# Attention on a Trainium2: masks multiplied on GpSimd, other products paced by the exponential of the step ahead, one Q half kept back

## The chip, the cores and the metric

One Trainium2 chip, eight cores, one program on all of them. Core number 4b+c works on batch b and on every fourth token from token c on, 1024 query tokens in all. The cores exchange nothing. The time is that of the slowest core, in microseconds (us) of the device.

## The reference, cut to what matters

```python
q = jnp.einsum('bse,hed->bhsd', x, Wq) + bq[None, :, None, :]      # 16 heads of 128
kg = jnp.einsum('bse,ged->bgsd', x, Wk) + bk[None, :, None, :]     # 4 groups
vg = jnp.einsum('bse,ged->bgsd', x, Wv) + bv[None, :, None, :]
k, v = jnp.repeat(kg, 4, axis=1), jnp.repeat(vg, 4, axis=1)
scores = jnp.einsum('bhqd,bhkd->bhqk', q, k) * (1.0 / np.sqrt(d))
scores = jnp.where(causal[None, None, :, :], -jnp.inf, scores)
attn = jax.nn.softmax(scores, axis=-1)
out = jnp.einsum('bhqk,bhkd->bhqd', attn, v)
# x = layernorm(x + out), with x of shape (2, 4096, 2048)
# x = fwht(x * SU_ug) / 64; silu(x @ W_gate.T * ..) * (x @ W_up.T * ..)
# x = fwht(x * SU_dp) / 64; x @ W_down.T * ..; layernorm(x + that)
```

## The kernel before, in words

Five stages follow each other on each core. K and V of the whole batch are projected first (until about 250 us), then comes attention (about 255 to 667 us), then the up and gate products with the second transform, then the down product with the last norm.

**Attention** runs in 384 steps. A head has two halves of 512 queries (`hf` 0 and 1). Half 0 has 8 steps, half 1 has 16; a step P takes 256 keys. The order of the halves is head after head, with (14, 0), (15, 0), (14, 1), (15, 1) at the end (`halves`, line 397). In the last 8 steps of each half the causal edge passes through the tile: step r of them (r = 0 to 7) works on the last 512-64r queries only. Step i of the program issues, in this order on TensorE:

- S(i): two score products of up to 512 columns (`emit_S`, line 418), into one of two pairs of PSUM banks. S(i) waits for the exponential of step i-2. ScalarE then takes the exponential of both (line 437), 1024 columns in a full step.
- O(i-3): the products of the probabilities with V (`emit_O`, line 454), up to eight of 129 columns; the last column sums the row. `LO` = 3 is the lag.
- "other products" (`run_items`, line 604), as many as a budget allows. Each step adds a quota to the budget, each product takes 1.0 off it.

After TensorE's part of a step comes, on the program's list, `out_bank` (line 472) where a pair of query tiles is finished (r = 3 and r = 7): VectorE's reciprocal, two multiply-adds, for r = 7 a cast, and two statistics. Then `emit_mask(i)` (line 441): 64 columns of each score tile are multiplied by the mask on VectorE (line 451), and for odd r GpSimd zeroes 64 more (line 449). O(i) waits for these.

**The other products** come from two queues. The plain one holds the projections of the Q halves still to come, 16 products of 512 columns each (`q_item`); Q of head h may start at the first step of head h-2. The `fast` one holds for each finished half a transpose (T: four products of 128 columns, `tr_mm`) and at least three steps after it the first transform (F: one product, `f1_mm`). These items use PSUM banks 6 and 7 in turn, so the first product of an item waits until VectorE has emptied the bank of the item before the last (`free[bk]`; line 371 for Q, 518 for T, 528 for F). Each engine works its list in order. Once the first halves of all heads are done, the statistics of the norm (`norm_A`) and 16 pairs of products with the stage matrix (`st1_mm`, emptied by line 585) join the queue. GpSimd's list also holds the loads of the weights of Q (line 359) and of up and gate (`ug_load`, line 633), which wait for TensorE to let go of the place. The first load of up and gate is issued when Q of (15, 1) is done.

## Time and profile before

| | us |
|---|---|
| median of 3 runs (2090.55 to 2092.16) | 2091.55 |
| the profiled execution | 2087.97 |
| its span, slowest core | 2086.9 |
| the eight cores' spans | 2077.2 to 2086.9 |
| TensorE busy in the span | 2021.6 (97%) |
| ScalarE, VectorE, GpSimd busy | 488.4, 566.4, 149.2 |

The profile is of one execution; TensorE is busy nearly always, and the chain of work that ended last runs 88% over it. Busy time of TensorE is partly modelled: products overlap, so a run of products is best read by its start and the start of what comes next. A wait is put down to the engine whose signal came last.

### The profile page before, as it was taken

To read this page: it belongs to the slowest core of one execution; us is meant where nothing else is said; L and a number is where in the kernel's file an instruction comes from. 1 tells how busy PE (TensorE), PEld (TensorE's weight loads), DVE (VectorE), ACT (ScalarE), POOL (GpSimd) and SP (SyncE) were. 2 spreads that over 40 slices of the span, in tenths; PEclk is the share of its full clock that TensorE was granted. 3 is DMA by queue.
4 is the path that set the end of the run, shared out by engine and by line. 5 is a ranking of instruction groups with operands and counts; after the bars stand their busy time and mean duration, and the time that the engine had idled before them with its cause. 6 is when DMAs were issued, how large, how long until landed. Compare 5 with 4: busy or idle time off the path is not lost.

```text
span 2086.9 us, 30398 instructions; the slowest of 8 cores (2077.2 to 2086.9 us)
## 1 busy us (share of the span) xinstructions
PE 2021.6 (97%) x11760; PEld 1043.6 (50%) x11760; DVE 566.4 (27%) x1334; ACT 488.4 (23%) x639; POOL 149.2 (7%) x364
## 2 busy tenths in 40 slices
PE   5999999999998999999999999999998999999997
PEld 2444466666665444444444444444444754444456
DVE  0111144445556412212212212122122530303033
ACT  0110088777785101001001001001002410000002
POOL 3000000000000000000000000000000000000001
PEclk9999999999999999999999999999999999999999
DMA  9885133333325355455455455455453743747359
GB/s 153 140 129 94 30 62 77 72 72 73 81 55 92 61 97 98 84 97 97 84 98 96 84 98 96 84 98 94 85 98 79 127 105 70 159 81 156 73 126 311
DMA packets 92812, 207.00 MB, mean 99 GB/s; under 512 B 11776, under 2 KB 51712, under 8 KB 87680
## 3 DMA queue, kind: packets, MB, share of 16 engines
q0 software_dynamic: 34816, 141.74, 39.3%
q1 hardware_dynamic: 57856, 63.32, 10.8%
q8 instruction: 97, 1.59, 0.3%
q14 instruction: 43, 0.35, 0.1%
HBM read 294.31 MB, written 24.12 MB: 153 GB/s over the span
## 4 chain that ended last, share of the span: by engine, by line
PE 88%; DMA 5%; DVE 2%; ACT 2%; issue 1%; POOL 1%; DVEq 0%; SPq 0%; ACTq 0%; POOLq 0%
PE PS L181 88%; DMA AR<-xkv 2%; ACT AR L437 2%; DMA AR<-scr_h 1%; DMA scr_h<-wmt 1%; POOL AR L219 1%; DMA AR<-WdownP 1%; DMA out<-AR 0%; DVE AR L484 0%; DVE AR L451 0%; DMA AR<-AR 0%; DVE AR L371 0%; DVE stat L882 0%; DVE stat L495 0%; DVE AR L528 0%
## 5 line engine op out<-in xcount | busy, mean ns | idle before, releaser
L181 PE MATMUL PS<-AR 128*128 128x512 bf16 (+4 forms) x11296 | 1979.0, 334 | 45.6 <-DMA AR<-WkT 21.0
L181 PEld LDWEIGHTS PS<-AR 128*128 128x128 bf16 x11296 | 1005.0, 98 | 994.5 <-issue 87.3
L437 ACT ACTIVATE AR<-PS,negc 128x1024 bf16<-128x1024 f32 (+7 forms) x384 | 322.8, 865 | 100.3 <-PE PS L181 91.1
L786 ACT ACTIVATE AR<-PS,sgate 128x512 bf16<-128x512 f32 x128 | 88.0, 687 | 825.5 <-PE PS L181 825.5
L790 DVE SCALAR_TENSOR_TENSOR AR<-PS,scombo,AR 128x512 bf16<-128x512 f32 x128 | 96.1, 751 | 445.4 <-ACT AR L786 445.4
L741 DVE CAST AR<-PS 128x512 bf16<-128x512 f32 x128 | 88.5, 692 | 276.0 <-PE PS L181 276.0
L635 POOL DMA_DIRECT2D AR<-WupT x64 | 33.8, 529 | 838.2 <-PE PS L181 838.2
L451 DVE TENSOR_TENSOR AR<-AR,maskb 128x128 bf16<-128x128 bf16 x256 | 52.3, 218 | 117.7 <-ACT AR L437 117.5
L891 DVE TENSOR_TENSOR a_b<-PS,AR 128x512 f32<-128x512 f32 (+1 forms) x16 | 9.7, 622 | 271.5 <-PE PS L181 267.8
L1000 ACT ACT_TABLE_LOAD x1 | 1.3, 1283 | 349.3 <-DVE mv L998 349.3
L276 DVE TENSOR_TENSOR AR<-PS,AR 128x512 bf16<-128x512 f32 x32 | 21.8, 690 | 221.0 <-PE PS L181 221.0
L271 ACT ACTIVATE AR<-PS,bkc 128x512 bf16<-128x512 f32 x32 | 21.7, 687 | 164.2 <-PE PS L181 164.2
L181 PE MATMUL PS<-AR,st 128*128 128x512 bf16 x160 | 53.7, 387 | 2.3 <-DVE AR L585 2.3
L845 DVE CAST AR<-PS 128x512 bf16<-128x512 f32 x64 | 44.1, 690 | 35.5 <-PE PS L181 35.5
L848 ACT CAST AR<-PS 128x512 bf16<-128x512 f32 x64 | 37.4, 586 | 52.8 <-PE PS L181 52.8
L181 PE MATMUL PS<-AR,h 128*128 128x512 bf16 x128 | 48.8, 381 | 0.0
L755 POOL DMA_DIRECT2D AR<-WdownP x32 | 16.9, 532 | 435.9 <-PE PS L181 398.5
L484 DVE SCALAR_TENSOR_TENSOR AR<-PS,rcp,AR 128x128 f32<-128x128 f32 x128 | 39.1, 346 | 8.5 <-DVE rcp L477 3.6
L449 POOL MEMSET AR<- 128x128 bf16 x128 | 25.2, 210 | 214.5 <-PE PS L181 214.4
L371 DVE TENSOR_SCALAR AR<-PS,bqc 128x512 bf16<-128x512 f32 x32 | 24.0, 749 | 43.1 <-PE PS L181 43.1
L636 POOL DMA_DIRECT2D AR<-WgateT x64 | 34.2, 534 | 3.1 <-issue 2.9
L495 DVE BATCH_NORM_STATS2 stat<-AR 128x6 f32<-128x128 f32 x128 | 30.9, 283 | 3.7 <-DVE AR L484 0.5
(72 smaller groups left out, 319.0 us busy)
## 6 DMA issues: line engine op xcount, KB each, us to landing
AR<-WupT POOLq DMA_DIRECT2D x64, 512.0 KB, 6.8
AR<-WgateT POOLq DMA_DIRECT2D x64, 512.0 KB, 11.0
AR<-WdownP POOLq DMA_DIRECT2D x32, 1024.0 KB, 10.2
AR<-AR SPq DMA_DIRECT2D x256, 64.0 KB, 4.9
AR<-xkv POOLq DMA_DIRECT2D x6, 2048.0 KB, 22.1
AR<-WqT POOLq DMA_DIRECT2D x16, 512.0 KB, 6.6
AR<-xtok SPq DMA_DIRECT2D x16, 512.0 KB, 4.3
scr_h<-AR SPq DMA_DIRECT2D x32, 256.0 KB, 2.3
```

Of the source, the lines that this page charges most:

```text
L181: return pe.matmul(o, lhsT, rhs, start=start, stop=stop, skip_group_check=True)
L437: et = p.inc(ac.activation(ebuf[:, :, cs:], sps[:, :, cs:], AF.Exp, bias=negc[:, 0:1], scale=INV_SQRT_D), "ac")
L451: e_tok[i][1] = p.inc(dv.tensor_tensor(ebuf[:, :, cs:cs + 64], ebuf[:, :, cs:cs + 64], mask2, ALU.mult), "dv")
L484: h1t = p.inc(dv.scalar_tensor_tensor(sl, ops[:, a, 0:D], rcp[:, 2 * ob + a: 2 * ob + a + 1], sl, ALU.mult, ALU.add), "dv")
L495: h1_half[n] = p.inc(dv.bn_stats(stat[:, o_:o_ + 6], x_[:, q * 128:(q + 1) * 128]), "dv")
L635: p.inc(gp.dma_start(wup[c % 3], WupT[c][:, :]), f"ug{c % 3}", 16)
L636: ug_tok[c] = p.inc(gp.dma_start(wgt[c % 3], WgateT[c][:, :]), f"ug{c % 3}", 16)
L741: free[bk] = t_ = p.inc(dv.tensor_copy(b1[s_], bank(bk)), "dv")
L786: at = p.inc(ac.activation(gsl[k], bank(2 + k), AF.Silu, bias=0.0, scale=sgate[:, c:c + 1]), "ac")
L790: t_ = p.inc(dv.scalar_tensor_tensor(av[k], bank(k), scombo[:, c:c + 1], gsl[k], ALU.mult, ALU.mult), "dv")
L845: acc_free[bk] = p.inc(dv.tensor_copy(bts(hf, j), bank(bk)), "dv")
L848: acc_free[bk] = p.inc(ac.copy(bts(hf, j), bank(bk)), "ac")
```

## The change

Three things are changed, all in attention. The mask product moves from VectorE's list to GpSimd's, behind the zeroing where there is one; O(i) then waits for one GpSimd signal. The quota is no longer a number between 1.15 and 1.70 but comes from `pace(i)`: an estimate of the exponential of step i-1, times `PACE` = 1.11, less an estimate of the step's own products, in units of one 512-column product; the last step of a half now runs its items at once too, where before it only saved its quota. And Q of (15, 1) may no longer start with head 13 but only with the half (14, 1).

```diff
-        LO = 3
+        LO, PACE = 3, 1.11
...
+                assert q_tok[h][hf]
                 p.w(pe, q_tok[h][hf])
...
-            e_tok[i] = [et, et, None]
+            e_tok[i] = [et, et]
...
             if r % 2:
                 p.w(gp, kv_done, o_tok[i - 6] if i >= 6 else None)
-                e_tok[i][2] = p.inc(gp.memset(ebuf[:, :, cs - 64:cs], 0.0), "pl")
-            p.w(dv, e_tok[i][0])
-            e_tok[i][1] = p.inc(dv.tensor_tensor(
-                ebuf[:, :, cs:cs + 64], ebuf[:, :, cs:cs + 64], mask2, ALU.mult), "dv")
+                p.inc(gp.memset(ebuf[:, :, cs - 64:cs], 0.0), "pl")
+            p.w(gp, e_tok[i][0], cw)
+            e_tok[i][1] = p.inc(gp.tensor_tensor(
+                ebuf[:, :, cs:cs + 64], ebuf[:, :, cs:cs + 64], mask2, ALU.mult), "pl")
...
+        def pace(i):
+            def cols(k):
+                return HT - steps[k][5] if 0 <= k < NS else 0
+            def tiles(k):
+                return 4 - max(steps[k][4], 0) // 2 if 0 <= k < NS else 0
+            if i >= NS:
+                return 0.0
+            exps = PACE * (0.26 + 0.83e-3 * 2 * cols(i - 1))
+            own = 2 * cols(i) * 0.42e-3 + 2 * tiles(i - LO) * 0.057
+            return max(0.0, (exps - own) / 0.2155)
...
-                q_item(h, hf, first_step[(max(h - 2, 0), 0)])
+                q_item(h, hf, first_step[(14, 1) if (h, hf) == (15, 1) else (max(h - 2, 0), 0)])
...
-            quota = 1.15 + 0.55 * (512 - steps[i][5]) / 512 if i < NS else 0.0
-            if i >= LO and steps[i - LO][7]:
-                emit_O(i - LO)
-                state["budget"] += quota
-            elif i > LO and steps[i - LO][6]:
+            quota = pace(i)
+            if i >= LO and steps[i - LO][6]:
                 emit_O(i - LO, (0,))
                 run_items(i, quota)
                 emit_O(i - LO, (1,))
```

How this moves instructions, at three places. First TensorE at the start of head 7's first half; 448, 384 and 320 columns are S of its steps 1 to 3, 129 columns are O, 512 columns a Q product. Before:

```order
L181 MATMUL PS<-AR 128x448 x2
L181 MATMUL PS<-AR 128x129 x2
L181 MATMUL PS<-AR 128x512 x2
L181 MATMUL PS<-AR 128x384 x2
L181 MATMUL PS<-AR 128x129 x2
L181 MATMUL PS<-AR 128x320 x2
L181 MATMUL PS<-AR 128x129 x4
L181 MATMUL PS<-AR 128x512 x3
```

Now:

```order
L181 MATMUL PS<-AR 128x448 x2
L181 MATMUL PS<-AR 128x129 x2
L181 MATMUL PS<-AR 128x512 x3
L181 MATMUL PS<-AR 128x384 x2
L181 MATMUL PS<-AR 128x129 x2
L181 MATMUL PS<-AR 128x512 x4
L181 MATMUL PS<-AR 128x320 x2
L181 MATMUL PS<-AR 128x129 x4
L181 MATMUL PS<-AR 128x512
```

Between S of 384 and S of 320 columns stood no Q product, now there are four.

Second VectorE in the middle of head 5, where the item Q of (6, 0) ends and F and T of earlier halves follow; L477 to L495 (L478 to L496 in the new numbering) are `out_bank`. Before:

```order
L477 RECIPROCAL rcp<-PS 128x2
L484 SCALAR_TENSOR_TENSOR AR<-PS,rcp,AR 128x128 x2
L495 BN_STATS stat<-AR 128x6 x2
L451 TENSOR_TENSOR AR<-AR,maskb 128x2x64
L371 TENSOR_SCALAR AR<-PS,bqc 128x512
L451 TENSOR_TENSOR AR<-AR,maskb 128x2x64
L528 CAST AR<-PS 128x512
L518 CAST AR<-PS 128x512
```

Now:

```order
L371 TENSOR_SCALAR AR<-PS,bqc 128x512
L478 RECIPROCAL rcp<-PS 128x2
L485 SCALAR_TENSOR_TENSOR AR<-PS,rcp,AR 128x128 x2
L496 BN_STATS stat<-AR 128x6 x2
L529 CAST AR<-PS 128x512
L519 CAST AR<-PS 128x512
```

The masks are gone, the emptying of Q's bank stands ahead of the `out_bank` group, and that of F's bank still behind it.

Third TensorE in the half (15, 0), steps 1 to 6. Before:

```order
L181 MATMUL PS<-AR 128x448 x2
L181 MATMUL PS<-AR 128x129 x2
L181 MATMUL PS<-AR 128x512 x2
L181 MATMUL PS<-AR 128x384 x2
L181 MATMUL PS<-AR 128x129 x2
L181 MATMUL PS<-AR 128x320 x2
L181 MATMUL PS<-AR 128x129 x4
L181 MATMUL PS<-AR 128x512 x3
```

Now:

```order
L181 MATMUL PS<-AR 128x448 x2
L181 MATMUL PS<-AR 128x129 x2
L181 MATMUL PS<-ident,AR 128x128 x2
L181 MATMUL PS<-AR 128x384 x2
L181 MATMUL PS<-AR 128x129 x2
L181 MATMUL PS<-AR 128x320 x2
L181 MATMUL PS<-AR 128x129 x8
L181 MATMUL PS<-AR 128x256 x2
L181 MATMUL PS<-AR 128x129 x8
L181 MATMUL PS<-AR 128x512
L181 MATMUL PS<-AR 128x192 x2
```

The 512-column products of Q (15, 1) have left this half; they now stand in (14, 1).

## Rows read from the trace of the kernel before

**Rows 1.** Spans of the cores: span from first to last instruction, granted clock.
```profile
core 0: 2085.2 us, clock 0.994
core 7: 2086.9 us, clock 0.993
```

**Rows 2.** Core 7 by stretch: length, then busy time and count per engine, clock.
```profile
250.00:670.00 420.00, 398.38 (x3786) 262.16 (x3784) 210.75 (x732) 323.22 (x386) 35.61 (x148) 0.99 0.34 76
720.00:1300.00 580.00, 580.00 (x2689) 262.99 (x2688) 117.64 (x164) 55.67 (x81) 43.34 (x83) 1.00 0.51 94
```

**Rows 3.** What TensorE waited for, 255 to 671 us, core 7: us, times, longest.
```profile
PE PS L181 <- DVE AR L451: 8.9, 12, 2.1
PE PS L181 <- ACT AR L437: 7.1, 22, 1.4
PE PS L181 <- DVE AR L371: 2.0, 6, 0.5
PE PS L181 <- DVE AR L585: 1.8, 1, 1.8
```

**Rows 4.** Groups by shape in attention: busy us, mean ns of one, idle before.
```profile
L437 ACT ACTIVATE AR<-PS,negc 128x1024 bf16<-128x1024 f32 x160 | 174.5, 1113 | 59.0 <-PE PS L181 58.9
L437 ACT ACTIVATE AR<-PS,negc 128x128 bf16<-128x128 f32 x32 | 11.8, 367 | 8.4 <-PE PS L181 6.2
L181 PE MATMUL PS<-AR 128*128 128x512 bf16 x853 | 244.5, 381 | 5.3 <-DVE AR L451 3.1 <-ACT AR L437 1.4 <-DVE AR L528 0.2
L181 PE MATMUL PS<-AR 128*128 128x129 bf16 x2304 | 198.4, 220 | 4.3 <-DVE AR L451 3.7 <-DVE AR L484 0.3
L451 DVE TENSOR_TENSOR AR<-AR,maskb 128x128 bf16<-128x128 bf16 x256 | 52.3, 218 | 117.7 <-ACT AR L437 117.5
L449 POOL MEMSET AR<- 128x128 bf16 x128 | 25.2, 210 | 214.5 <-PE PS L181 214.4
L359 POOL DMA_DIRECT2D AR<-WqT x16 | 8.5, 531 | 226.9 <-PE PS L181 226.9
```

**Rows 5.** Timeline, head 7: start, us, engine, instruction, idle before and releaser.
```profile
438.22 5.18 PE L181 MATMUL PS<-AR 128*128 128x320 bf16 x56 [0.30 <-ACT AR L437]
...
442.35 0.75 DVE L371 TENSOR_SCALAR AR<-PS,bqc 128x512 bf16<-128x512 f32 x1 [0.33 <-PE PS L181]
...
444.95 0.68 DVE L528 CAST AR<-PS 128x512 bf16<-128x512 f32 x1
445.55 0.21 DVE L451 TENSOR_TENSOR AR<-AR,maskb 128x128 bf16<-128x128 bf16 x1
...
445.77 2.64 PE L181 MATMUL PS<-AR 128*128 128x512 bf16 x8 [2.14 <-DVE AR L451]
```

**Rows 6.** Timeline, head 5, in the middle between its halves.
```profile
391.09 0.17 DVE L477 RECIPROCAL rcp<-PS 128x2 f32<-128x2 f32 x1
...
392.14 0.49 DVE L495 BATCH_NORM_STATS2 stat<-AR 128x6 f32<-128x128 f32 x2
...
392.67 0.74 DVE L371 TENSOR_SCALAR AR<-PS,bqc 128x512 bf16<-128x512 f32 x1
...
393.56 0.33 PE L181 MATMUL PS<-ident,AR 128*128 128x128 bf16 x3 [0.99 <-DVE AR L451]
```

**Rows 7.** Timeline, head 6: a mask and the product that waits for it.
```profile
419.13 0.21 DVE L451 TENSOR_TENSOR AR<-AR,maskb 128x128 bf16<-128x128 bf16 x1
...
419.48 0.27 PE L181 MATMUL PS<-AR 128*128 128x129 bf16 x2 [0.76 <-DVE AR L451]
```

**Rows 8.** Timeline, half (14, 1) and the end of attention.
```profile
639.89 2.79 PE L181 MATMUL PS<-AR 128*128 128x448 bf16 x30 [1.38 <-ACT AR L437]
...
666.26 0.61 PE L181 MATMUL PS<-AR 128*128 128x129 bf16 x4 [1.76 <-DVE AR L451]
...
669.52 0.59 PE L181 MATMUL PS<-AR,st 128*128 128x512 bf16 x1 [1.79 <-DVE AR L585]
```

**Rows 9.** Core 7, 5 us of head 7, columns as in rows 2.
```profile
445.00:450.00 5.00, 4.22 (x18) 2.10 (x19) 2.09 (x7) 2.17 (x3) 0.00 (x0) 0.66 0.09 26
```

## The prediction

> **What bounds the kernel now.** I read the spans of the cores first, then busy time by stretch, then what TensorE waited for in attention, then the groups by shape, and last the timeline around the longest waits. Eight cores do equal work and differ by under 10 us; the slowest, core 7, has 2086.9, core 0 has 2085.2 [rows 1]. After attention TensorE is busy without a gap: 580.00 of 580 us, which also gives the pitch of a 512-column product, 580/2689 = 0.216 us [rows 2]. In attention it is busy for 398.4 of 420 us [rows 2]. The change adds and takes no product, so all it can win there is the 21.6 us of idle time, 1.0% of the span, and what the clock does. I price other products by their columns: O of 129 columns 0.054 us (the kernel's own figure is 0.057, which I use), S of 64 columns 0.027.
>
> The idle time has three parts. VectorE's masks are named for 8.9 us in 12 waits, ScalarE's exponentials for 7.1 in 22, the emptying of Q's bank for 2.0 in 6, and one wait of 1.8 stands at the end [rows 3]. ScalarE is busy for 323 of the 420 us [rows 2], so it is not the bound on average; a full exponential takes 1.11 us, the smallest 0.37 [rows 4], and a step of TensorE must hold that much work or TensorE waits two steps later.
>
> **Who is really waited for.** The name of the mask is wrong in more than half of the 8.9 us. In head 6 a mask ends at 419.13 + 0.21 = 419.34 and the O product starts at 419.48, 0.14 later [rows 7]: that is what a signal takes. In head 7 the mask ends at 445.76 and TensorE starts at 445.77, too soon for that signal; F's bank was emptied at 444.95 + 0.68 = 445.63, 0.14 before [rows 5]. The product that starts is the first of a Q item, and the bank it needs is F's. The same in head 5: L371 ends at 393.41, T starts at 393.56 [rows 6]. By shape, 3.7 of the 8.9 us stand before O products, which do wait for masks; 3.1 stand before 512-column products and the rest, 2.1, before transposes [rows 4], which wait for banks. So before: masks 3.7, banks 5.2 + 2.0 + 0.2 = 7.4, exponentials 7.1, the end 1.8.
>
> **Masks to GpSimd.** 256 products leave VectorE, 52.3 us of work [rows 4]; VectorE does not end the chain, so this counts only through who waited. No row shows a two-input product on GpSimd. Below, it costs no less than GpSimd's zeroing of the same 128 elements, 0.21; above, I bound it by twice GpSimd's longest instruction in the stretch, the issue of a weight load of 0.53, so 1.06 [rows 4]. I take 0.43, the zeroing plus VectorE's own product (0.21 + 0.22), since the op writes as the one and reads as the other. O(i) stands behind S(i+2), which itself waits for exponential i, and behind S(i+3); with the signals that leaves at least some 0.6 us after the exponential, so at 0.43 nobody waits. In the list the masks stand behind one weight load per head, whose wait for TensorE is over by then, and a load issues in 0.53 us; with a mask due each 0.4 to 1.1 us and three steps of lag this is hidden too. The waits before O go, 3.7 us, but for 0.4 at the very end, where mask and O follow the last exponential with nothing between: -3.3 us. At that end 1.76 is now shown because two masks stood behind `out_bank` [rows 8].
>
> The GPSIMD Engine Reference of the Trainium skill (Performance versus the Vector engine, elementwise) speaks against the move: about 2.6 cycles an element for two inputs against VectorE's one, roughly half VectorE's rate. By its figures I estimate 128 x 2.6 / 1.2 GHz = 0.28 us and some dispatch. By that rule too the product would be hidden and the sum would be the same; no row of before shows it.
>
> **Pacing.** In step 2 of a half nothing but S and one pair of O stood between two full exponentials: steps 1 and 2 of the first half held 0.92 + 0.44 us against exponentials of 1.11 and 1.0. Hence the wait of 0.30 before S of 320 columns in each first half [rows 5] and its like. Now three or four products stand there, 1.14 + 1.30 us in head 7. Of the 7.1 us I let go all but the first steps of attention (0.5) and the 1.38 of half (14, 1) [rows 8], which is halved because three queue items now reach it. It costs elsewhere: half (15, 0) loses its Q products. Its steps 1 to 7 hold 4.1 us of products against 5.5 of exponentials (seven of them, from 1.11 down to 0.47 in even steps of 0.107, [rows 4]), so 1.5 with the signals. Sum 0.5 + 0.7 + 1.5, rounded up to 3.0: -4.1 us.
>
> **The banks: what is late next.** Pacing also places T, F and Q anew, and here it loses. Take the middle of head 5, from the end X of the step that ends Q of (6, 0). Its bank is read 0.24 later (a product takes 0.38 [rows 4] against a pitch of 0.216, and a signal) and is free at 0.99. Then comes `out_bank`, which lasts from 391.09 to 392.63, 1.54 us [rows 6]: until 2.53. F's bank takes 0.68 [rows 5]: 3.21, and 0.14 for the signal: 3.35. TensorE reaches Q of (6, 1), which needs F's bank, after S and O and F (0.50), S and O (0.66), and S, O and T (0.77): 1.93. It waits 1.42 us. The same walk in the order of before puts T's wait at 0.92, and the trace has 0.99 [rows 6], so I trust it to 0.2 or so. For the other heads it gives: heads 1 and 2, where F, T and the next Q item now stand in one step, 1.0 each (before, F and Q were 2.2 us apart); head 3 1.2; head 4 1.4; head 6 1.0. Together 7.0. In heads 7 to 13 both Q's and F's bank are now emptied ahead of `out_bank`: T is 0.95 us behind a bank that takes 1.13, 0.18 each, 1.3 together, where before head 7 alone had 2.14 [rows 5]. The items in the second halves follow each other at 0.94 to 1.05 us against 1.05 to 1.13, 1.7 together. Sum 10.0 against 7.4: +2.6 us.
>
> **The end and the clock.** The 1.79 before the stage products is VectorE's emptying of banks behind `out_bank` [rows 8] and stays. On core 7 the granted clock was 0.66 in the five microseconds after the 2.14 wait [rows 9]: 3.4 us at 1.2 instead of 2.4 GHz, 1.7 us of work lost. My longest wait there is now 1.42, and after 1.38 and 0.99 before no such fall is in the stretch's rows, so I take it to be gone: -1.7 for core 7. Core 0, at 2085.2 without that loss, is then level with it.
>
> **Sum.** -3.3 - 4.1 + 2.6 - 1.7 = -6.5 us: span 2086.9 to 2080.4. The profiled execution took 2087.97, the median of the runs is 2091.55; I carry the difference over to the median: 2085.0.
>
> **Rivals.**
> 1. The banks get no worse. VectorE has 52 us less to do, and if `out_bank` starts or runs earlier than in my walk, or TensorE arrives later, the 7.0 us shrink towards 1. For it: the walk counts microseconds that hang on steps of 0.1; against: it met the 0.99. Gain 6.5 + 6 = 12.5: 2079.
> 2. Nothing is left of it: the waits in the middle of heads 1 to 6 reach 2 us each (a multiply-add that is late for its reciprocal), or the clock falls in them or in the thin half (15, 0), 1.7 us a time, twice. For it: 2.14 did bring a fall [rows 9]. +5.5: 2090.5.
> 3. GpSimd becomes the bound, and the kernel slower. Eight masks and four zeroings of 0.21 per half must fit in the eight steps' 6.6 us (1.11 times eight exponentials of 0.74 on average) and some 1.5 of lag. 8T + 0.84 = 8.1 at T = 0.91: below that price of a mask no throughput is lost, above it 8 us for each microsecond, in 32 halves. At the upper bound, 1.06, 1.2 us a half, 39 in all: 2124. Against it: 1.06 is five times either nearest row. If instead T lies between 0.6 and 0.9, single O products wait a tenth or two, and this joins rival 2.
> 4. The change does not pace as it says, because the items run out as before. The lists show otherwise in the first steps of the halves, so I give it nothing of its own.
>
> **How the numbers follow.** Forecast 0.50, with its own range 2081 to 2088.5; rival 1 0.20; rival 2 0.20; rival 3 0.06; 0.04 for slower by another way. What a measurement of this kernel can tell from no change is about 0.2%, 4.2 us, so faster is below 2087.4. Faster: 0.43 of the forecast's 0.50 and rival 1's 0.20, 0.63. Within: 0.07 and 0.17 of rival 2, 0.24. Slower: the remaining 0.13. The range 2077 to 2091.5 leaves out rival 3, the far end of rival 1 and part of rival 2.
>
> **What would show it.** In the waits of TensorE the mask's line should be nearly gone (under 1 us), ScalarE's line should be about 3 us with the longest pieces near 630 us in half (15, 0), and the emptying lines of Q's and F's banks should be named for some 10 us, with waits of 1.0 to 1.5 in the middle of heads 1 to 6 and under 0.3 in heads 7 to 13. GpSimd's product should have a mean of about 0.43. If that mean is over 0.9, or the waits of a head's middle are gone or at 2 us, the prediction is wrong at that step. Rows after attention should be as before, only earlier.

## The result, and the profile after

The changed kernel takes 2069.7 us, median of 4 runs (2068.67 to 2070.28), against 2091.53 (2090.55 to 2092.16): ratio 0.9899, 95% interval 0.9887 to 0.9911. It is 21.8 us faster. 6.5 were forecast, and 2069.7 lies below the range of 2077 to 2091.5. In some executions of either kernel the cores of one die run at a lower granted clock and take longer; they are left out of all times and stages here. The profiled execution took 2069.54; its cores have 2058.1 to 2068.5 us, and the slowest is now core 4, not 7.

Core 4 by stretch (columns as in rows 2):

```profile
250.00:670.00 420.00, 408.38 (x3834) 268.45 (x3833) 180.70 (x495) 326.95 (x390) 139.10 (x404) 0.99 0.32 77
720.00:1300.00 580.00, 580.00 (x2689) 262.91 (x2688) 117.11 (x163) 55.71 (x82) 43.32 (x82) 1.00 0.48 93
```

Against [rows 2] TensorE is busy for 10 us more of the 420, VectorE for 30 us less, GpSimd for 103 more. After attention nothing has changed. What TensorE still waited for between 250 and 675 us on core 4:

```profile
PE PS L181 <- DVE AR L529: 3.5, 7, 1.1
PE PS L181 <- DMA AR<-AR: 2.0, 1, 2.0
PE PS L181 <- DVE AR L586: 1.7, 1, 1.7
PE PS L181 <- ACT AR L438: 1.2, 3, 0.5
PE PS L181 <- DVE AR L371: 1.2, 3, 0.5
PE PS L181 <- DVE AR L485: 0.6, 2, 0.3
...
PE PS L181 <- POOL AR L452: 0.3, 1, 0.3
```

Against [rows 3]: masks 8.9 to 0.3, exponentials 7.1 to 1.2. The two groups on GpSimd, in attention:

```profile
L452 POOL TENSOR_TENSOR AR<-AR,maskb 128x128 bf16<-128x128 bf16 x256 | 110.7, 434 | 163.2 <-ACT AR L438 121.3 <-PE PS L181 38.3
L450 POOL MEMSET AR<- 128x128 bf16 x128 | 26.6, 208 | 0.0
```

434 ns is the price that the prediction took. The longer waits of TensorE, one by one (timeline, columns as in rows 5):

```profile
288.67 0.38 PE L181 MATMUL PS<-ident,AR 128*128 128x128 bf16 x4 [0.31 <-DVE AR L371]
289.30 2.00 PE L181 MATMUL PS<-AR 128*128 128x512 bf16 x10 [0.25 <-DVE AR L529]
...
363.39 0.81 PE L181 MATMUL PS<-AR 128*128 128x512 bf16 x3 [1.12 <-DVE AR L529]
...
604.20 0.60 PE L181 MATMUL PS<-AR 128*128 128x384 bf16 x4 [0.53 <-ACT AR L438]
605.10 1.11 PE L181 MATMUL PS<-AR 128*128 128x320 bf16 x8 [0.30 <-ACT AR L438]
...
629.97 0.38 PE L181 MATMUL PS<-AR,st 128*128 128x512 bf16 x1 [1.99 <-DMA AR<-AR]
...
651.64 0.58 PE L181 MATMUL PS<-AR,st 128*128 128x512 bf16 x1 [1.71 <-DVE AR L586]
```

The waits stand where they were forecast: before Q of the second half in the middle of a head (363.39, head 4), in the thin half (15, 0) (604.20, 605.10), and before the emptying at the end (651.64). One was not: the first stage product now comes so early that it waits 1.99 us for the DMA that scatters the F of the half before it.

**Measured by starts.** The shown waits of attention fell by some 9 us, which does not account for 21.8. So I took the *starts* of products instead of the idle time between records. A product of 512 columns starts 0.216 us after the one before [rows 2], but its record lasts 0.38 [rows 4], so a record ends about 0.165 after the engine could go on. The rows show each wait short by that much, and none below it. For each product of attention I took start less the start before less its columns' time (the gap before a product, mean of the six cores whose records are all there; us):

| | S, for the exponential | O | T, F, Q, for banks | end | sum | attention |
|---|---|---|---|---|---|---|
| before | 14.5 | 6.8 | 12.5 | 2.6 | 36.5 | 406.5 |
| changed | 4.7 | 2.5 | 10.1 | 5.0 | 22.2 | 391.3 |
| forecast, from the rows | 7.1 to 3.0 | 3.7 to 0.4 | 7.4 to 10.0 | 1.8 to 1.8 | | |

"End" stands for the products of the norm and the stage matrix; it includes waits behind the last O (1.9 us before), which the last column leaves out. The last column is the mean over the cores from the first product of attention to its last O. The stage ahead of it, from the first product of all, fell too: 248.7 to 243.2 us. So attention gave 15.2 us and the first stage 5.5, 20.7 together. The later stages agree to 0.6 each, and all that is left took 1.4 us longer: the mean span of the cores fell by 19.3 us between these two profiles, that of the slowest core by 18.4. The 21.8 is between medians; the profiled execution before, 2087.97, was 3.6 us below its median. The Perfetto Trace Analysis of the Trainium skill (Summary: the profiler window per engine type) says that TensorE's records end at an estimated end, and its opening note calls matmul busy time a bad metric since matmuls are pipelined. This trace agrees, with the 0.38 against 0.216.

### The profile page after: what moved, and what is told of

Same layout as the page of the kernel before. It is cut to its first block, busy times and chain, and to the rows that moved or that the text cites. A ratio compares the mean times of both kernels' runs of the same rounds, so it can differ in the third digit from the quotient of the medians.

```text
span 2068.5 us, 30358 instructions; the slowest of 8 cores (2058.1 to 2068.5 us)
## 1 busy us (share of the span) xinstructions
PE 2016.6 (97%) x11760; PEld 1043.9 (50%) x11760; DVE 527.7 (26%) x1078; ACT 489.7 (24%) x639; POOL 252.4 (12%) x620
## 4 chain that ended last, share of the span: by engine, by line
PE 91%; DMA 5%; DVE 2%; issue 1%; POOL 1%; ACT 0%; DVEq 0%; SPq 0%; ACTq 0%; POOLq 0%
PE PS L181 91%; DMA AR<-xkv 2%; DMA AR<-scr_h 1%; POOL AR L219 1%; DMA scr_h<-wmt 1%; DMA AR<-WdownP 1%; DMA out<-AR 0%; DMA AR<-AR 0%; DVE AR L529 0%; DVE stat L896 0%; DVE AR L371 0%; DVE AR L485 0%; ACT AR L438 0%; DVE a_b L914 0%; DVE wmt L914 0%
## 5 line engine op out<-in xcount | busy, mean ns | idle before, releaser
L452 POOL TENSOR_TENSOR AR<-AR,maskb 128x128 bf16<-128x128 bf16 x256 | 110.7, 434 | 163.2 <-ACT AR L438 121.3
L276 DVE TENSOR_TENSOR AR<-PS,AR 128x512 bf16<-128x512 f32 x32 | 21.8, 691 | 217.1 <-PE PS L181 217.1
L769 POOL DMA_DIRECT2D AR<-WdownP x32 | 16.9, 531 | 435.6 <-PE PS L181 435.6
L496 DVE BATCH_NORM_STATS2 stat<-AR 128x6 f32<-128x128 f32 x128 | 30.8, 282 | 3.3
L478 DVE RECIPROCAL rcp<-PS 128x2 f32<-128x2 f32 x64 | 10.7, 167 | 70.8 <-PE PS L181 70.8
```

The costliest lines, as they stand in the source:

```text
L452: e_tok[i][1] = p.inc(gp.tensor_tensor(ebuf[:, :, cs:cs + 64], ebuf[:, :, cs:cs + 64], mask2, ALU.mult), "pl")
L496: h1_half[n] = p.inc(dv.bn_stats(stat[:, o_:o_ + 6], x_[:, q * 128:(q + 1) * 128]), "dv")
```

## The experiments

All numbers of stages are means over the cores of one profile, by starts. "First" is the stage before attention; the last column counts instructions in TensorE's list, the program that the engine works through in order, waits included. "Late half" is Q of (15, 1) held back to (14, 1); "filler" is a small instruction that does nothing useful. Two profiles of the same kernel, before, differ by 0.7 us in the first stage and 0.4 in attention.

| kernel | first | attention | TensorE's list |
|---|---|---|---|
| before | 248.7 | 406.5 | 13246 |
| before, again | 249.4 | 406.9 | 13246 |
| masks on GpSimd alone | 245.0 | 403.1 | 13215 |
| pacing and late half alone | 249.7 | 405.0 | 13248 |
| changed, without the late half | 244.3 | 391.5 | 13213 |
| changed | 243.2 | 391.3 | 13210 |
| before, last mask on GpSimd | 250.3 | 406.7 | 13245 |
| before, zeroing three times | 250.2 | 406.4 | 13246 |
| changed, filler on VectorE | 245.0 | 392.9 | 13210 |
| the same, longer | 243.3 | 393.2 | 13210 |
| changed, 36 waits on TensorE | 249.4 | 391.6 | 13246 |
| before, wait for zeroing on VectorE | 243.7 | 406.8 | 13118 |
| changed, mask twice | 244.7 | 432.8 | 13210 |
| changed, mask in two halves | 242.6 | 392.1 | 13210 |
| filler that waits for the exponential | 244.8 | 396.1 | 13210 |
| the same, and O waits for it | 249.6 | 404.6 | 13376 |
| out_bank a step later | 243.8 | 389.3 | 13214 |
| and the last one behind the stage products | 243.4 | 388.9 | 13213 |
| two steps later, stage products later | 243.3 | 386.6 | 13213 |
| the same with PACE 1.25 | 244.2 | 396.3 | 13203 |

### The parts alone

The kernel before, unchanged, on the chip of the next three:

> The kernel before, unchanged, profiled once more. In the two profiles so far the first stage (first product to the start of attention, mean of the eight cores) took 248.7 us before and 243.2 us after, attention 406.5 and 391.3 us, though the change does not touch the first stage. If the 5.5 us of the first stage are chance, this profile has a first stage anywhere between 242 and 250 us, and attention again within 1 us of 406.5. If they belong to the kernel, the first stage is again 248 to 250 us.

2091.2 us, first stage 249.4: it belongs to the kernel and not to the execution.

```diff
 # before, masks alone
-            p.w(dv, e_tok[i][0])
-            e_tok[i][1] = p.inc(dv.tensor_tensor(
-                ebuf[:, :, cs:cs + 64], ebuf[:, :, cs:cs + 64], mask2, ALU.mult), "dv")
+            p.w(gp, e_tok[i][0], cw)
+            e_tok[i][1] = p.inc(gp.tensor_tensor(
+                ebuf[:, :, cs:cs + 64], ebuf[:, :, cs:cs + 64], mask2, ALU.mult), "pl")
```

> Only the mask products move to GpSimd; the quota and the start of Q (15, 1) are those of before. Theory 1 (pacing brings most): counted from start to start of the products, before has 36 us of waits in attention: 14.4 before score products, 6.5 before O, 12.5 at the banks of the other products, 2.6 at the end. The masks account for the 6.5 (down to 2.5) and for 1 to 2 of the banks: attention 400 to 402 us instead of 406.5, ratio 0.9975. Theory 2 (VectorE's relief brings most: with 52 us less in its list its banks come free early): attention 395 or less, ratio 0.994 or less.

Ratio 0.9948 (0.9935 to 0.9962). Attention fell by 3.4 us only.

```diff
 # before, with pace(i) and the late half of the change; the masks stay on VectorE
-            quota = 1.15 + 0.55 * (512 - steps[i][5]) / 512 if i < NS else 0.0
+            quota = pace(i)
```

> Only the pacing and the late Q (15, 1); the masks stay on VectorE. Theory 1: the waits before score products fall from 14.4 to about 5, those before O stay at 6 to 7, the banks stay near 12: attention 396 to 398 us, ratio 0.995. Theory 2: 403 or more, ratio 0.998 or more, since VectorE's list is as full as before.

Ratio 0.9989 (0.9980 to 0.9998). Attention fell by 1.5 us. The 403 or more of theory 2 was met here, but its 395 or less with the masks alone was not (403.1), and theory 1 missed both. So neither theory stands: neither half brings it. The longest listed waits of the two, core 4; masks alone, then pacing alone:

```profile
PE PS L181 <- ACT AR L437: 9.2, 29, 1.4
PE PS L181 <- DVE AR L371: 4.1, 10, 0.9
PE PS L181 <- DVE AR L528: 3.3, 4, 1.7
...
PE PS L181 <- POOL AR L451: 0.5, 1, 0.5
```

```profile
PE PS L181 <- DVE AR L452: 13.4, 21, 1.0
...
PE PS L181 <- ACT AR L438: 0.3, 1, 0.3
```

With the masks gone TensorE waits for the exponentials (by starts 16.9 us before S, 1.4 before O); with the pacing alone it waits for masks (2.3 before S, 22.3 before O). Each takes away the wait that would have hidden the other: 3.4 and 1.5 apart, 15.2 together. Some 18.5 of the 22.3 us stand before O of one step, r = 6: its mask is listed behind `out_bank` of r = 3, three steps earlier. How it stands in the second run (timeline, the middle of head 5, as [rows 6]):

```profile
389.56 0.37 ACT L438 ACTIVATE AR<-PS,negc 128x128 bf16<-128x128 f32 x1
...
390.19 0.16 DVE L478 RECIPROCAL rcp<-PS 128x2 f32<-128x2 f32 x1
...
391.23 0.49 DVE L496 BATCH_NORM_STATS2 stat<-AR 128x6 f32<-128x128 f32 x2
391.63 0.21 DVE L452 TENSOR_TENSOR AR<-AR,maskb 128x128 bf16<-128x128 bf16 x1
391.76 0.69 DVE L529 CAST AR<-PS 128x512 bf16<-128x512 f32 x1
391.99 0.27 PE L181 MATMUL PS<-AR 128*128 128x129 bf16 x2 [0.99 <-DVE AR L452]
```

The mask runs as soon as `out_bank` is through and ends at 391.84; O starts 0.15 later. It is the mask of r = 6; at 389.56 the exponential of r = 7 starts, so that of r = 6 was done, and the mask, 0.21 us of work, starts 2.07 us later than it could have, behind the emptying of Q's bank and `out_bank`.

```diff
 # changed, without the late half
-                q_item(h, hf, first_step[(14, 1) if (h, hf) == (15, 1) else (max(h - 2, 0), 0)])
+                q_item(h, hf, first_step[(max(h - 2, 0), 0)])
```

> The changed kernel, but Q of (15, 1) may start with head 13 as before. Theory 1: half (15, 0) has its Q products back and loses its waits before score products (1.5 to 2 us), half (14, 1) runs thin instead and gets a wait of 1.4 us or more there; the sum within 1 us of the changed kernel, 2069 to 2072 us. Rival: the late Q is what keeps TensorE's clock up at the end of (14, 1), where before a wait of 1.54 us stood; then this kernel is 2 to 4 us slower than the changed one.

2072.0 us, ratio 0.9913 (0.9887 to 0.9938), attention 391.5: the late half brings 0.2 us there, less than two profiles of one kernel differ by. The total is 2.3 us above the changed kernel's, as the rival has it, but 1.1 of them lie in the first stage, and the intervals of the two ratios overlap.

### What in the masks on VectorE cost it

```diff
 # changed; filler on VectorE at the mask's place (0.06 us each)
+            p.w(dv, rcp_free[0])
+            rcp_free[0] = p.inc(dv.memset(rcp[:, 0:2], 1.0), "dv")
             p.w(gp, e_tok[i][0], cw)
```

> The changed kernel, with one small memset of two columns on VectorE in the place where each of the 256 mask products stood; GpSimd keeps the masks. Theory A (the kind on GpSimd) and theory B1 (the length of GpSimd's list): the first stage stays at 243 to 245. Theory B2 (the shorter list of VectorE decides): 248 to 250. In attention it measures what it costs to keep VectorE's list at its old length with only some 0.06 us of work an instruction: if what the change won came from the exponentials that VectorE no longer has to wait for in its list (a mask cannot be taken before its exponential), the filler, which waits for no exponential, costs at most 2 us of the 15.3: attention 391 to 394.

2074.0 us, ratio 0.9912 (0.9891 to 0.9934); attention +1.6, within the 391 to 394 expected.

```diff
 # the filler waits for the exponential, as the mask did
-            p.w(dv, rcp_free[0])
+            p.w(dv, e_tok[i][0], rcp_free[0])
```

> The changed kernel, masks on GpSimd, with a small memset (0.06 us) on VectorE in the place of each mask, which now waits for the exponential of its step as the mask did; nothing waits for the memset. The same memset without that wait left attention at 392.9 us. Masks on VectorE with the new pacing took 405.0. Theory H (VectorE standing before an exponential holds up the emptying of banks and out_bank behind it, and that was half of what the masks cost): attention 396 to 400, with the waits for Q's, T's and F's banks grown from 10 us to 14 or more. Theory M (it was the mask that was late, behind out_bank in VectorE's list, with TensorE's O waiting for it): attention 392 to 394, banks within 1 us. First stage 243 to 245 by both, as TensorE's list keeps 13210 instructions.

Ratio 0.9930 (0.9901 to 0.9959); attention 396.1, +3.2 more. The time is that of theory H, its place is not: the waits for Q's, T's and F's banks rose by 0.7 us only, those before O by 3.3. They stand before the first O of a half (by starts 1.6 us in the run before this one, 4.7 now), which waits until `out_bank` has read the O bank of an earlier half: VectorE, standing before an exponential, holds up `out_bank`. That is the mechanism of theory H, at another bank.

```diff
 # and O waits for the filler
+            e_tok[i].append(rcp_free[0])
```

> As the last one, and O of the step waits for VectorE's memset as it waited for the mask there; GpSimd still does the masks, so VectorE has 0.06 us an item in place of 0.22. Theory M: TensorE's O waits for VectorE's list again, attention 402 to 405, with 18 to 22 us before O products; what the move to GpSimd won is then that the signal for O no longer stands behind out_bank, and not VectorE's 52 us of work. Theory W (it was the work of 0.22 us each): attention 393 to 396. TensorE's list is 13376 instructions long by these waits, so by the finding of the earlier runs the first stage should be 248 to 251.

Ratio 0.9992 (0.9980 to 1.0004): the whole gain is gone though GpSimd does every mask. Attention 404.6, 21.3 us before O, 16.7 of them at r = 6; theory M holds. Core 4, its waits and the same place as above:

```profile
PE PS L181 <- DVE rcp L452: 13.4, 22, 1.2
```

```profile
390.89 0.27 PE L181 MATMUL PS<-AR 128*128 128x129 bf16 x2 [0.89 <-DVE rcp L452]
```

From 391.3 to the 405.0 of the masks on VectorE under pacing: 1.6 for one more instruction in the list, 3.2 for its wait for the exponential, 8.5 for O's waiting on it, and 0.4 for the mask's greater work, no more than two profiles of one kernel differ by. In another order the parts could come out otherwise, but the greater work is at most a small one. What the move to GpSimd buys is a short list for a signal that TensorE waits on.

### The price of a mask on GpSimd

```diff
 # mask twice
+            t_ = p.inc(gp.tensor_tensor(
+                ebuf[:, :, cs:cs + 64], ebuf[:, :, cs:cs + 64], mask2, ALU.mult), "pl")
+            p.w(gp, t_)
```

> The changed kernel, with each mask product on GpSimd done twice, so that a masked tile costs GpSimd 2 x 0.434 = 0.87 us in place of 0.43. The prediction's rival 3 put the point at which GpSimd becomes the bound at 0.91 by throughput and said that single O products wait a tenth or two between 0.6 and 0.9. By that theory attention goes from 391.3 to some 395 to 400, with waits of TensorE named after the mask's line in the last steps of the halves. The other theory, that three steps of lag hide this as well: attention stays within 1 us of 391.3 and the total within 2 us of 2069.7.

2111.7 us, ratio 1.0091 (1.0073 to 1.0109): attention +41.5, against both theories. GpSimd's timeline in a masked stretch, core 0:

```profile
470.11 0.43 POOL L452 TENSOR_TENSOR AR<-AR,maskb 128x128 bf16<-128x128 bf16 x1
470.68 0.43 POOL L455 TENSOR_TENSOR AR<-AR,maskb 128x128 bf16<-128x128 bf16 x1
471.07 0.43 POOL L452 TENSOR_TENSOR AR<-AR,maskb 128x128 bf16<-128x128 bf16 x1
471.64 0.43 POOL L455 TENSOR_TENSOR AR<-AR,maskb 128x128 bf16<-128x128 bf16 x1
472.00 0.20 POOL L450 MEMSET AR<- 128x128 bf16 x1
472.17 0.43 POOL L452 TENSOR_TENSOR AR<-AR,maskb 128x128 bf16<-128x128 bf16 x1
```

It never rests. From start to start a tile costs 0.57 + 0.39 = 0.96. The last 8 steps of one head and the first 8 of the next are all masked, so 16 follow each other: from the first mask to the last 15 x 0.96 + 8 x 0.17 = 15.8 us (measured 15.7 to 16.7), where the changed kernel has 12.1 to 13.2. That is 3.6 more a head; from the last mask to the next first one it takes 1.0 less (0.8 in heads 7 to 13); 2.6 x 15 = 39 of the 41.5. Rival 3 counted a half by itself with a lag of its own, 13 us at this price by its formula.

```diff
 # mask in two halves of 64 columns
-            e_tok[i][1] = p.inc(gp.tensor_tensor(
-                ebuf[:, :, cs:cs + 64], ebuf[:, :, cs:cs + 64], mask2, ALU.mult), "pl")
+            for k in range(2):
+                e_tok[i][1] = p.inc(gp.tensor_tensor(
+                    ebuf[:, k:k + 1, cs:cs + 64], ebuf[:, k:k + 1, cs:cs + 64],
+                    mask2[:, k:k + 1, :], ALU.mult), "pl")
```

> The changed kernel with each mask product on GpSimd as two of 64 columns in place of one of 2 x 64. Doubled in full it cost 0.96 us a masked tile (0.57 + 0.39 from start to start) and 41.5 us of attention, since 16 masked steps follow each other: 16 x 0.96 + 8 x 0.17 of zeroing = 16.7 us in a stretch that lasts about 13.2. By that count the limit is at (13.2 + 1.5 of lag - 1.4) / 16 = 0.83 us a tile. If the price goes by elements with a small fixed part, two halves cost about 0.5 to 0.6 us: attention within 1 us of 391.3. If the fixed part is most of it, they cost 0.8: attention 391 to 396 with single waits. If the limit was really near 0.6, attention is over 396 already at 0.6.

Ratio 0.9899 (0.9872 to 0.9926). Attention 392.1 (cores 4 to 7), within 1 us. Its mask products on GpSimd, core 4:

```profile
L453 POOL TENSOR_TENSOR AR<-AR,maskb 128x64 bf16<-128x64 bf16 x512 | 148.6, 313 | 129.5 <-ACT AR L438 127.4
```

64 elements take 313 ns, 128 take 434: a line through the two has 0.19 us fixed and 1.9 ns an element. The GPSIMD Engine Reference of the Trainium skill (Performance versus the Vector engine, elementwise) has about 2.6 cycles an element, by its 1.2 GHz an estimated 2.2 ns; the measured is a little better. The two halves start 0.27 us apart, so a tile costs some 0.54. The price at which GpSimd becomes the bound lies between 0.54 and 0.96 us a tile.

### The first stage

With masks on GpSimd the first stage was 4 to 6 us shorter, though it has the same instructions and GpSimd issues its first 34 loads, until 19 us, at the same times. What differs is how they land: each piece is moved in 16 parts, and in the kernel before the last one comes 3.6 us after the fourteenth (mean of 24 pieces, eight cores), in the changed kernel 1.6. The bytes moved by 60 us are the same within 1%. The whole loss is there when the first block's products end: the 128th product starts 46.7 us after the first in the kernel before, 41.9 in the changed one.

```diff
 # before, one mask (the very last step's) on GpSimd
-            p.w(dv, e_tok[i][0])
...
+            eng, nm = (gp, "pl") if i == NS - 1 else (dv, "dv")
```

> The kernel before, with a single mask product, that of the very last step of attention, on GpSimd. What is asked is the first stage, up to the first attention product: 248.7 to 249.7 us (mean of the cores) in the three kernels with all masks on VectorE, 243.2 to 245.0 in the three with all on GpSimd, though the instructions of that stage are the same. Theory A (it is enough that GpSimd has a two-input product in its program at all): 243 to 245. Theory B (it goes by how the length of the engines' lists places things in memory): 248 to 250. Attention keeps its 406.5 by both, the total 2091 under B, 2086 under A.

```diff
 # before, the zeroing three times, each waiting for the one before
+                for _ in range(3):
                     e_tok[i][2] = p.inc(gp.memset(ebuf[:, :, cs - 64:cs], 0.0), "pl")
```

> The kernel before, with GpSimd's zeroing done three times in place of once: 256 more instructions in GpSimd's list, none of them a two-input product, and VectorE's list untouched. Theory A (the kind of the instruction decides the first stage): 248 to 250. Theory B1 (the length of GpSimd's list decides): 243 to 245. Attention: the zeroing of 0.21 us becomes 0.63 and is issued before the exponential ends, so it should stay hidden and attention stays at 406 to 407.

250.3 and 250.2 us: neither the kind of instruction nor the length of GpSimd's list, which the second makes 640 instructions longer with its waits (its ratio 0.9997, 0.9985 to 1.0009; the first has one execution, 2092.6 us). The single fillers above kept 245.0; a longer list of VectorE:

```diff
 # changed with the filler, doubled in the first three halves
-            p.w(dv, rcp_free[0])
+            for _ in range(2 if n < 3 else 1):
+                p.w(dv, rcp_free[0])
```

> The changed kernel with the small memset on VectorE for each mask, and two in place of one in the first three halves: VectorE's list is now 2664 instructions long, waits included, against 2652 of before and 2616 in the run with single fillers, which kept the short first stage (245.0 us). What is asked is the first stage alone. Theory P (the 5 us of the first stage come from where the lists lie in memory, which changes with their length, and the single fillers stayed a few dozen instructions under the point): 248 to 251. Theory K (it is bound to the masks being on GpSimd and not to the length of VectorE's list): 243 to 245. Attention 393 by both.

243.3 (one execution, 2070.7 us): VectorE's list is not it either.

```diff
 # changed, 36 waits on TensorE that are long met
             if i >= 2:
                 p.w(pe, e_tok[i - 2][0])
+            if i % 10 == 5 and i < 365:
+                pe.wait_ge(p.h["pe"], 1)
             else:
                 p.w(pe, kv_ac, kv_dv)
```

The `else` now belongs to the new line; its waits, for K and V, are in the list once, at the first step, as before, so that the list grows by the 36 alone.

> The changed kernel with 36 waits on TensorE that are met long before, one each in 36 steps of attention: TensorE's list is then 13246 instructions long, as long as before (with the masks on VectorE it needed 36 waits more than with the masks on GpSimd), against 13210 in the changed kernel. Theory P2 (the length of TensorE's list decides the first stage): 248 to 251 us. Theory K: 243 to 245. Attention 391 to 394 by both, for the waits themselves.

249.4, ratio 0.9922 (0.9901 to 0.9944): the long stage is back, and the fourteenth-to-last lag with it (3.4 us). With the masks on VectorE O waits for three engines, with the masks on GpSimd for two: 36 waits fewer in TensorE's list. The converse, in the kernel before:

```diff
+                zt, e_tok[i][2] = e_tok[i][2], None
+                p.w(dv, zt)
             p.w(dv, e_tok[i][0])
```

> The kernel before, masks on VectorE and the old quota; only the wait for GpSimd's zeroing is taken by VectorE's mask product in place of TensorE's O. TensorE's list falls from 13246 instructions to 13118, VectorE's grows from 2652 to 2780. Theory P2 (with a list of TensorE at 13246 or more the first stage takes 248 to 250 us, at 13215 or less 243 to 245; 36 idle waits alone turned the one into the other): first stage 243 to 246, attention 406 to 407, total some 2086. Theory K2 (the first stage is short only with the masks on GpSimd, and the 36 waits did harm in another way): 248 to 250, total 2091.

2084.8 us, ratio 0.9970 (0.9959 to 0.9981), first stage 243.7, attention as before. VectorE's list grew by the 128 instructions that TensorE's lost, so it is not the sum of the lists. GpSimd's fourth load of x, which waits for the first block's products, core 0, in the kernel before, the changed one, the one with 36 waits, and this one:

```profile
59.98 0.53 POOL L233 DMA_DIRECT2D AR<-xkv  x1 [40.30 <-PE PS L181]
```

```profile
54.47 0.53 POOL L233 DMA_DIRECT2D AR<-xkv  x1 [34.77 <-PE PS L181]
```

```profile
57.09 0.53 POOL L233 DMA_DIRECT2D AR<-xkv  x1 [37.41 <-PE PS L181]
```

```profile
50.94 0.53 POOL L233 DMA_DIRECT2D AR<-xkv  x1 [31.25 <-PE PS L181]
```

In all 20 profiles the stage has 248.7 to 250.3 us with 13245 instructions or more in TensorE's list and 242.6 to 245.0 with 13215 or fewer. That the list of TensorE decides is shown in both directions. Whether it is a length that must not be passed or a place in the list that comes back with every so many instructions, no run tells, and by what path it slows one or two of the sixteen parts of each load is open.

### Towards a better one

```diff
 # changed; out_bank of r = 3 a step later
-                if r in (3, 7):
-                    out_bank(n, h, hf, r // 4, o_tok[i - LO])
+                for fn in late:
+                    fn()
+                late.clear()
+                if r == 3:
+                    late.append(lambda a=(n, h, hf, 0, o_tok[i - LO]): out_bank(*a))
+                elif r == 7:
+                    out_bank(n, h, hf, 1, o_tok[i - LO])
```

> The changed kernel, with the out_bank group of the first pair of tiles (r = 3) issued one step later, behind what the step's items put on VectorE. Theory 1 (the 1.28 us before Q in heads 4 and 5, and the 0.4 to 0.7 before T and Q in heads 1 to 3 and 6, are F's and Q's banks being emptied behind out_bank): these waits go but for the 0.2 of a product's end and a signal, attention 391.3 to some 386, total 2065. Theory 2 (the emptying is late by its own 0.7 us and not by its place, or the late out_bank is now in the way of the next bank): attention 391 to 393, total 2070.

2069.3 us, ratio 0.9898 (0.9877 to 0.9919), attention -2.0 where 5 were expected. In heads 4 and 5 the 1.28 us are gone, so the place of `out_bank` was their cause. In heads 1 and 2 it now stands between the two emptyings, and the waits there grew from 0.88 to 1.57 us by starts (core 0):

```profile
287.07 0.75 DVE L371 TENSOR_SCALAR AR<-PS,bqc 128x512 bf16<-128x512 f32 x1 [2.78 <-PE PS L181]
...
287.74 0.16 DVE L478 RECIPROCAL rcp<-PS 128x2 f32<-128x2 f32 x1
...
289.19 0.67 DVE L529 CAST AR<-PS 128x512 bf16<-128x512 f32 x1
...
290.01 1.35 PE L181 MATMUL PS<-AR 128*128 128x512 bf16 x7 [1.40 <-DVE AR L529]
```

```diff
 # and the very last out_bank behind the stage products
+                elif r == 7 and i == NS + LO - 1:
+                    late.append(lambda a=(n, h, hf, 1, o_tok[i - LO]): out_bank(*a))
...
+        for fn in late:
+            fn()
```

> As the last one, and the very last out_bank group of attention stands behind the emptying of the last stage products. Theory 1 (the 1.7 to 1.9 us at the end, which both kernels have, are VectorE's emptying behind out_bank): 1.5 us less than the last one, attention some 384.5, total 2063.5. Theory 2 (what follows attention waits for out_bank, or the end is then bound by the emptying itself, 0.6 us each): no gain, total as the last one.

2064.5 us, ratio 0.9875 (0.9860 to 0.9891). Attention and the stage behind it took 2.5 us less than in the last: the 1.7 were `out_bank` at the end.

```diff
-                for fn in late:
-                    fn()
-                late.clear()
-                if r == 3:
-                    late.append(lambda a=(n, h, hf, 0, o_tok[i - LO]): out_bank(*a))
+                if late and late[0][0] <= i:
+                    late.pop(0)[1]()
+                if r == 3:
+                    late.append((i + 2, lambda a=(n, h, hf, 0, o_tok[i - LO]): out_bank(*a)))
...
-                add_item(lastA + 17 + j, 2.0, [lambda bk, j=j: st1_mm(0, j, bk)],
+                add_item(lastA + 20 + j, 2.0, [lambda bk, j=j: st1_mm(0, j, bk)],
```

> As the kernel with the late bank group and the changed end (2064.5 us), with the first out_bank group two steps late in place of one, and the stage products allowed three steps later. Theory 1 (in heads 1 and 2 the group now stands ahead of F's bank because F comes two steps behind Q; the wait of 2.6 before the first stage product is for the DMA that scatters F of the half before it): the 1.57 in heads 1 and 2 and the 2.6 go, less some 1 us at the end because more stage products stand there: attention 388.9 to some 385, total 2061. Theory 2 (the products not issued there leave the steps of (15, 1) without work, so the wait is only named otherwise): within 1 us of 388.9.

2063.3 us, ratio 0.9871 (0.9849 to 0.9894), the fastest of all, though not told apart from the last. The 2.6 us before the stage products became 0.75; the 1.57 in heads 1 and 2 stayed, since the group only moved from one place ahead of F's emptying to another.

```diff
-        LO, PACE = 3, 1.11
+        LO, PACE = 3, 1.25
```

> As the last one with PACE = 1.25 in place of 1.11: more other products in the steps with much exponential, and the items of a head run out earlier, so that later steps have none. (At 1.08 and below, Q of a head is not done when it is wanted.) Theory 1 (at 1.11 what is left of the waits for the exponential, 4.4 us, stands in the first steps of attention and in (15, 0), where no pace helps): no better, and 2 to 6 us worse for the steps that find no item. Theory 2 (a larger margin absorbs signals and spread): 1 to 2 us better.

2070.4 us, ratio 0.9922 (0.9880 to 0.9964): attention +9.7, and with the stages behind it +7. The items run out: by starts S waits 12.6 us. The longest piece, 1.8, stands in (14, 1), others of 0.5 to 0.8 in (13, 1), (14, 0), (15, 0) and (15, 1).

## Why the prediction was wrong, step by step

**"All it can win there is the 21.6 us of idle time."** This is the step that failed first. By starts the kernel before had some 33 us over its products' own time in attention (406.5 against some 373: 3,735 products which, where nothing is waited for, start 0.216 us apart with 512 columns, 0.109 with 256 and 0.057 with 129), and the change takes 15.2 of them. The pitch stood in the prediction, from the same rows; it was used to price products and not to count what they should take in all.

**Pacing, -4.1.** It measured 14.5 to 4.7, -9.8. The after side was near (4.7 for 3.0; the pieces in (15, 0) 1.15 for 1.5). The before side, 7.1, was half of the truth: 22 listed waits were each short by some 0.17, and those under it were not there at all.

**Masks, -3.3.** 6.8 to 2.5, -4.3, for the same reason. The price of 0.43 held, in part by luck: it was the sum of two other instructions' times, and its two parts measured 0.19 fixed and 0.24 for the elements. The argument that it is hidden held. But "VectorE does not end the chain, so this counts only through who waited" took who waited in the old order. Under the new one O would have waited 22.3 us for VectorE. The terms were summed as if they were independent; alone they give 3.4 and 1.5.

**Banks, +2.6.** The walk gave 10.0 and 10.1 were measured, head by head too: 1.4 forecast and 1.28 found in heads 4 and 5, 1.0 and 0.88 in heads 1 and 2, 0.18 and 0.22 in heads 7 to 13; head 6 missed (1.0, found 0.54). That the sums agree to 0.1 is partly luck: the middle of heads 1 to 6 has 5.9 for 7.0, heads 7 to 13 1.5 for 1.3, and the rest 2.6 for 1.7. Against a true 12.5 before, the term's sign turns: -2.4.

**The end, 0.** The wait behind `out_bank` stayed (1.79, now 1.71). The stage product that waits for the DMA that scatters F was not seen: +2.4 in all. The prediction asked what a faster engine triggers only for the banks.

**The clock, -1.7.** On core 7 the fall at 445 is gone. Of before-type executions, cores with that fall took 407.1 us in attention and those without it 405.9, so it was worth 1.2. On core 4, the slowest now, the row after the scatter's wait has 0.66:

```profile
629.00:634.00 5.00, 4.03 (x14) 1.68 (x15) 1.94 (x3) 1.54 (x2) 0.54 (x2) 0.66 0.55 76
```

The prediction also left out the fall that follows the last waits of attention. Behind them the granted clock was at half for 3.4 or 6.8 us on every core before, 6.0 in the mean, and for 3.0 in the mean in the changed kernel, where two cores have none.

**The first stage** had no term, since no instruction in it changed. 5.5 us came there, with the shorter list of TensorE.

The terms as measured by starts (-9.8, -4.3, -2.4 and +2.4, in which the clock's loss is contained, and -5.5 for the first stage) come to -19.6; the sum had -6.5.

**Rivals.** Rival 1 (banks no worse) named a place that did not change; the size it gave, 12.5, came nearest only by chance. Rival 3's mechanism exists: at 0.96 us a tile it costs 41.5 us, three times the 13 of its formula, since 16 masked steps adjoin. The measured 0.43 is under its limit. Of rival 2, no wait in the middle of a head passed 1.28, but core 4 had a fall of the clock at 630, behind the wait for the scatter, which it did not name. Rival 4 is out: the waits for the exponential fell as the pacing meant them to.

## What to carry to other kernels

Measure the room of a stage as its length less its products' columns at the pitch, and waits from start to start; idle time between records shows each wait short by a product's tail (0.165 us here) and hides the small ones. Before adding the gains of two edits, ask which wait of the one was hidden behind that of the other: a paced order needs every signal that TensorE waits on to come from a list in which nothing long stands ahead of it. And where a stage changes in which no instruction does, compare the lengths of the engines' lists too: here one list's length was the reason.

## What the runs showed of the hardware that was not expected

- 36 more instructions in TensorE's list, all of them waits that are met and stand in another stage, made the first stage, whose start is bound by loads, 6 us longer (13210 to 13246 instructions, 243.2 to 249.4 us), and a list shortened from 13246 to 13118 in the other kernel made it 5 us shorter (248.7 to 243.7).
- GpSimd's two-input product: 0.19 us fixed and 1.9 ns an element (313 ns for 64, 434 for 128), 0.39 from start to start when nothing is waited for and 0.57 when it waits for the one before (128 elements).
- VectorE's memset of two columns takes 0.06 us, and 256 of them, for which no other engine waits, still cost 1.6 us in attention (391.3 to 392.9).
